# A four-block state-space and expert layer on one core: decay denominators from TensorE, dt spread by DMA, sums inside the last pairs, matrices on VectorE

## What is computed

```python
dt = clip(softplus(dt_raw + dt_bias), 1e-4, 0.1)             # per token and head
A = (pi * sigmoid(theta_raw)) ** 2 ; kdamp = 0.5 * sigmoid(k_raw)   # per head and state
denom = 1.0 + dt * kdamp + dt ** 2 * A
v = (v - dt * A * y + dt * u * Bv) / denom
y = y + dt * v + dt * u * By
o = sum_n(y * Cy) + sum_n(v * Cv)
```

## Time and profile before

| what | us |
|---|---|
| median of 3 runs (549.52 to 549.85) | 549.67 |
| the profiled execution | 547.52 |
| its span, first to last instruction | 545.8 |
| busy: TensorE, VectorE | 444.1, 469.8 |
| busy: ScalarE, GpSimd | 252.1, 306.3 |

### The profile page before, as it was taken

One profiled execution on the slowest core, in us unless ns is written; L12 is line 12 of the kernel. 1 busy time (PEld: TensorE's weight loads), 2 busy tenths in 40 slices (PEclk: granted clock), 3 DMA queues, 4 the chain that ended last, 5 costly groups with the idle time before them and its releaser, 6 DMA issues. The chain is left out here.

```text
span 545.8 us, 9581 instructions
## 1 busy us (share of the span) xinstructions
PE 444.1 (81%) x3238; PEld 358.6 (66%) x3238; DVE 469.8 (86%) x1275; ACT 252.1 (46%) x489; POOL 306.3 (56%) x373
## 2 busy tenths in 40 slices
PE   5850159996979988896889968898789987998997
PEld 4740147885747667784657757687565766786886
DVE  5699989989999998989989998989989997789542
ACT  1551126563375525453546524454537542444363
POOL 2027867768508757668526657676553676778100
PEclk9995559998999969999979988998988997999999
DMA  7500000000000010000000000000000000000000
GB/s 224 153 0 0 1 1 2 1 2 1 0 1 1 1 40 1 1 1 2 1 0 2 0 21 1 1 2 2 0 1 0 2 0 21 2 1 1 2 11 10
DMA packets 8434, 7.06 MB, mean 13 GB/s; under 512 B 1593, under 2 KB 7618, under 8 KB 8258
## 3 DMA queue, kind: packets, MB, share of 16 engines
q1 hardware_dynamic: 8386, 6.46, 3.9%
HBM read 5.41 MB, written 1.05 MB: 12 GB/s over the span
## 5 line engine op out<-in xcount | busy, mean ns | idle before, releaser
L590 PE MATMUL BC<-xnT,winT 128*128 128x128 f32 x512 | 79.8, 306 | 50.8 <-ACT pr L893 29.7
L590 PEld LDWEIGHTS BC<-xnT,winT 128*128 128x128 f32 x512 | 70.4, 214 | 58.2 <-issue 31.0
L1616 POOL TENSOR_TENSOR big<-mm 128x256 f32<-128x256 f32 x64 | 50.3, 786 | 71.4 <-DVE mm L1345 71.4
L1648 POOL TENSOR_SCALAR uT<-uT,skipT 128x512 f32<-128x512 f32 x8 | 17.0, 2138 | 73.9 <-DVE w L1430 42.1
L1619 POOL TENSOR_TENSOR vt<-mm 128x256 f32<-128x256 f32 x64 | 58.1, 907 | 0.0
L542 PE MATMUL HB<-xnT,w 128*128 128x512 f32 x108 | 55.7, 645 | 1.9 <-ACT gtm L978 0.9
L1637 POOL TENSOR_TENSOR mm<-ab,pr 128x256 f32<-128x256 f32 x48 | 41.3, 881 | 20.4 <-ACT pr L893 20.2
L915 ACT ACTIVATE big<-GV 128x256 f32<-128x256 f32 x60 | 23.1, 385 | 62.3 <-PE GV L615 60.9
L612 PE MATMUL GV<-big,vt 128*128 128x128 f32 x256 | 44.0, 297 | 8.3 <-POOL vt L1619 8.3
L1343 DVE TENSOR_TENSOR mm<-BC,pr 128x512 f32<-128x512 f32 x64 | 44.2, 691 | 5.7
L612 PEld LDWEIGHTS GV<-big,vt 128*128 128x128 f32 x256 | 35.8, 202 | 14.1 <-POOL vt L1619 11.6
(11 more groups left out here) (225 smaller groups left out, 1179.1 us busy)
## 6 DMA issues: line engine op xcount, KB each, us to landing
xr<-in_x SPq DMA_DIRECT2D x4, 256.0 KB, 4.5
winT<-in_w_inT SPq DMA_DIRECT2D x1, 1024.0 KB, 5.6
w<-in_rw SPq DMA_DIRECT2D x1, 1024.0 KB
out<-xr SPq DMA_DIRECT2D x3, 256.0 KB, 2.6
taps<-in_dw_wT SPq DMA_DIRECT2D x1, 512.0 KB, 3.6
w<-in_sw SPq DMA_DIRECT2D x2, 128.0 KB
out<-xr SPq DMA_DIRECT2D x2, 128.0 KB, 1.8
winT<-in_w_inT SPq DMA_DIRECT2D x1, 130.0 KB, 2.7
```

The costliest lines, as they stand in the source:

```text
L590: last = pe.matmul(b[:, j * TS:(j + 1) * TS], winT[:, col:col + NS], xt, start=True, stop=True)
L1616: pool.tensor_tensor(wt[q % 8][:], m[:, 0], m[:, 3], ALU.add)
```

## The change

1. The transpose at F_ROWS takes dt and its square together: `dtts` holds (tile, {dt, dt squared}, head), one more VectorE operation squares dt, four transposes put them into 8 rows of 512 tokens, and ScalarE copies these into `rows8`.
2. For each head (F_DENS = 9 to 12, block 0 too) one matmul of 8 rows and 512 columns against `coef8` gives `kdamp*dt + A*dt*dt` on all 128 partitions. ScalarE takes the logarithm right from PSUM into `lden`. The products L1151 and L1146, the copies L830, L832 and L820, and the logarithm L842 are gone.
3. `coef8` is made once at the start: a transpose of kdamp and A (`kavec`), a mask, and four VectorE operations.
4. dt itself, which beta and alpha of blocks 1 to 3 read from `ab`, comes by DMA: SyncE writes the four rows to a DRAM buffer and reads them back to all partitions, four transfers of 256 KB. Block 0 still takes it from matmuls of identity columns, four of 512 columns, now after the denominators' four.
5. The constants move: the running sums to k = 14 and 15, `inverse_den` from k = 18 to 16, `running_den` and beta from 19 to 17, alpha from 21 to 19.
6. GpSimd's `matrices` is gone; VectorE does all 20 operations in every block, where it did 16 in blocks 1 to 3.

```diff
-MAT_OPS = 14
+MAT_OPS = 20
-F_INV, F_BETA, F_DEN, F_ALPHA = KP + 2, KP + 3, KP + 3, KP + 5
-
-(F_STATS, F_XN, F_XNT, F_LOGITS, F_EXP, F_LOG1P, F_ROWS, F_BCAST, F_LOG, F_SCAN, F_CENTRE) = (
-    0, 2, 3, 5, 6, 7, 8, 9, 13, 15, 17)
+F_INV, F_BETA, F_DEN, F_ALPHA = KP, KP + 1, KP + 1, KP + 3
+
+(F_STATS, F_XN, F_XNT, F_LOGITS, F_EXP, F_LOG1P, F_ROWS, F_DENS, F_SCAN, F_CENTRE) = (
+    0, 2, 3, 5, 6, 7, 8, 9, 14, 16)
...
+            def spread_dt(g):
+                sp.wait_ge(h_free, h_read_of("rows", g))
+                if g > 1:
+                    sp.wait_ge(ld_dt, 16 * NH * (g - 1))
+                sp.dma_start(dt_rows, rows8[0:NH]).then_inc(st_dt, 16)
+                sp.wait_ge(st_dt, 16 * g)
+                sp.wait_ge(fill, FILL_OPS * g)
+                sp.wait_ge(fill_p, POOL_FILL_OPS * g)
+                sp.wait_ge(mat_d, MAT_OPS * g)
+                for h in range(NH):
+                    sp.dma_start(view(ab, DTN + h * SL, (NH * SL, GT), (1, TS)),
+                                 dt_rows[h:h + 1].rearrange("o (c t) -> o c t", c=GT).broadcast_to([128, GT, TS]))\
+                        .then_inc(ld_dt, 16)
...
-                    pe.transpose(hb[0:KP, 0:TS], dtts[g % 2][:], ident[:]).then_inc(h_ready, 1)
+                    for c in range(GT):
+                        last = pe.transpose(hb[0:2 * NH, c * TS:(c + 1) * TS],
+                                            dtts[g % 2][:, c].rearrange("p i h -> p (i h)"), ident[:])
+                    last.then_inc(h_ready, 1)
...
-                    for c in range(GT):
-                        row = NH * c + h
-                        last = pe.matmul(hb[:, c * TS:(c + 1) * TS], ident[0:KP, row:row + 1].broadcast_to([KP, 128]),
-                                         dtr, start=True, stop=True)
+                    hb = h_bank("den", g, h)
+                    pe.matmul(hb[:], coef8[:, h, :], rows8, start=True, stop=True).then_inc(h_ready, 1)
...
+            for h in range(NH):
+                pe.matmul(DT0[h][:], ident[0:2 * NH, h:h + 1].broadcast_to([2 * NH, 128]), rows8,
+                          start=True, stop=True).then_inc(first_dt, 1)
...
-                    act.activation(den_of(h), hb[:].rearrange("p (c f t) -> p c f t", c=GT, f=2), ACT.Identity,
-                                   bias=kvec[:, h:h + 1], scale=avec[:, h:h + 1])
-                    act.activation(view(ab, DTN + h * SL, (NH * SL, GT), (1, TS)), by_tile(hb[:]), ACT.Copy)\
+                if 0 <= k - F_DENS < NH:
+                    hb = h_read("den", g, h)
+                    act.activation(den_of(h), hb[:].rearrange("p (c f t) -> p c f t", c=GT, f=2), ACT.Ln, bias=1.0)\
                         .then_inc(h_free, 1)
...
-            def denominators(g, h):
-                dve.wait_ge(h_free, h_read_of("bcast", g, h))
-                dve.tensor_tensor(den_of(h), den_of(h), view(ab, DTN + h * SL, (NH * SL, GT), (MID, 2), (1, MID)),
-                                  ALU.mult).then_inc(den_done, 1)
...
             def beta(g):
                 dve.wait_ge(inv_den, NH + g)
+                dve.wait_ge(ld_dt, 16 * NH * g)
...
-            def matrices(g):
-                pool.wait_ge(ab_done, g + 1)
-                pool.wait_ge(h_ready, h_read_of("sums", GT * g - 1))
-                link(pool.tensor_tensor(scr_x(0), c1(0, 1), c2(0, 0), ALU.mult))
-                link(pool.tensor_scalar(entry(0, "x", "x"), scr_x(0), -1.0, 1.0, ALU.mult, ALU.add))
-                link(pool.tensor_tensor(scr_x(0), c2(0, 1), entry(0, "x", "x"), ALU.mult))
-                pool.tensor_tensor(entry(0, "v", "x"), c2(0, 0), scr_x(0), ALU.add).then_inc(mat_p, 1)
...
-                    matrices(g + 1)
                     rstd_of(ln_index(LN2, g))
```

More of the change, by code:

```diff
@@ L124, in build @@
         theta = sb("theta", NS, NH)
-        avec = sb("avec", NS, NH)
-        kvec = sb("kvec", NS, NH)
+        kavec = sb("kavec", NS, 2 * NH)
+        kvec, avec = kavec[:, 0:NH], kavec[:, NH:2 * NH]
+        head_mask = sb("head_mask", 2 * NH, NH)
+        coef8 = sb("coef8", 2 * NH, NH, NS)
         sgt = sb("sgt", NS, 4 * NH)
@@ L147, in build @@
         rstd = sb("rstd", 128, GT)
-        dtts = [sb(f"dtt{i}", 128, KP) for i in range(2)]
+        dtts = [sb(f"dtt{i}", 128, GT, 2, NH) for i in range(2)]
         lden = sb("lden", NS, 2 * KP * MID)
@@ L204, in build @@
         einv = sb("einv", 128, GT)
-        cmp, tie = (t[:].rearrange("p (c e j) -> p c e j", c=GT, e=NE) for t in tf)
+        cmp, tie = (t.rearrange("p (c e j) -> p c e j", c=GT, e=NE) for t in tf)
         rank = sb("rank", 128, GT, NE)
@@ L245, in build @@
         inv_den, beta_done = sem("inv_den"), sem("beta_done")
-        first_dt, first_id = sem("first_dt"), sem("first_id")
-        mat_f, mat_p, mat_d, mat_e, step, conv, fill, fill_p = (sem(s) for s in
-            ("mat_f", "mat_p", "mat_d", "mat_e", "step", "conv", "fill", "fill_p"))
+        first_dt = sem("first_dt")
+        mat_d, step, conv, fill, fill_p = (sem(s) for s in ("mat_d", "step", "conv", "fill", "fill_p"))
         bc_ready, sq_done, vc_done, mul_done, wv_done = (sem(s) for s in
@@ L1246, in matrices @@
             def matrices(g, part):
                 def after(n):
-                    dve.wait_ge(mat_d, MAT_OPS * (g - 1) + n)
+                    dve.wait_ge(mat_d, MAT_OPS * g + n)
                 if part == 0:
                     dve.wait_ge(ab_done, g + 1)
-                    dve.wait_ge(wv_done, KP * g)
-                    dve.wait_ge(h_ready, h_read_of("sums", GT * g - 1))
+                    if g:
+                        dve.wait_ge(wv_done, KP * g)
+                        dve.wait_ge(h_ready, h_read_of("sums", GT * g - 1))
@@ L1269, in matrices @@
+                    for f in range(2):
+                        after(5 + f)
                         dve.tensor_tensor(scr(f, 0), c1(f, 1), scr(f, 1), ALU.mult).then_inc(mat_d, 1)
-                    after(6)
-                    dve.tensor_tensor(scr_x(1), c2(1, 1), entry(1, "x", "x"), ALU.mult).then_inc(mat_d, 1)
+                    for f in range(2):
+                        after(7 + f)
+                        dve.tensor_tensor(scr_x(f), c2(f, 1), entry(f, "x", "x"), ALU.mult).then_inc(mat_d, 1)
@@ L1279, in matrices @@
                     for f in range(2):
-                        after(10 + f)
+                        after(11 + f)
+                        dve.tensor_tensor(entry(f, "v", "x"), c2(f, 0), scr_x(f), ALU.add).then_inc(mat_d, 1)
+                    for f in range(2):
+                        after(13 + f)
                         dve.tensor_tensor(scr(f, 0), c2(f, 1), entry(f, "x", "v"), ALU.mult).then_inc(mat_d, 1)
                     for f in range(2):
-                        after(13 + f)
@@ L1483, in _ @@
             last.then_inc(taps_done, 1)
-            for k in range(F_XNT, F_BCAST):
-                front_early(0, k)
-            first_denominators(0)
-            for h in range(1, NH):
-                first_denominators(h)
-                head_sums(h - 1)
-            head_sums(NH - 1)
+            dve.wait_ge(cst_g, 1)
+            link(dve.tensor_tensor(head_mask[:], ident[0:2 * NH, 0:NH], ident[0:2 * NH, NH:2 * NH], ALU.add))
+            dve.wait_ge(coef_t, 1)
+            for h in range(NH):
+                last = dve.tensor_scalar(coef8[:, h, :], RR[0:2 * NH, 0:NS], head_mask[:, h:h + 1], None, ALU.mult)
+            last.then_inc(coef_done, 1)
+            for k in range(F_XNT, F_DENS):
+                front_early(0, k)
+            for h in range(NH):
+                head_sums(h)
             head_coefficients()
-            first_matrices()
+            for part in range(3):
+                matrices(0, part)
             for g in range(NG):
```

130 lines of the change are left out of this document (42 added, 88 removed).

## The result

The changed kernel takes 562.67 us (median of 6 executions, 561.51 to 566.59), the kernel before 549.72 beside it: a ratio of 1.0247 (1.0213 to 1.028). On a second chip it was 565.99 against 549.2, 1.0315 (1.0289 to 1.0341). It is slower, as forecast, but by 13 to 17 us and not by 6.8. The profiled execution is the longest of the six, 566.59.

A forecast was written before the change was run, and what follows sets the result against it. VectorE was busiest (469.8 of 545.8 us), with TensorE the bound in pairs 8 to 13. Start -0.7 plus three blocks of +2.5 gave +6.8 on 549.67: 556.5 us, range 540 to 563.

The forecast's parts named there:

- the steps at 3.55 a block: Tail of a block: from -0.9 us at the end of state(2) to +2.65 at residual(3), through the moved steps.
- The start: Start of block 0: denominators by wide matmuls, -0.7 us; bounds +0.7 at the slow clock throughout, -1.4 without waiting for TensorE.
- the clock rise "near 27.5": Start of block 0: TensorE's clock rises near 27.5 us, so the last bank comes near 29.3 and VectorE ends near 31.0.
- Pairs 8 to 14: Each block's pairs 8 to 14: TensorE bounds, most of VectorE's removed 4.2 us becomes waiting; -0.9 at state(2)'s end.
- The faster rival: Pairs 8 to 13: TensorE isn't the bound, so 5.4 us a block more is gained; 540.3 us, chance 0.20.
- DMA: Moving the dt rows through DRAM costs nothing: the transfers end by 124 us and beta starts at 138.24.
- The order of the tail: Last pair and tail: first sum ahead of pair 15, exponentials ahead of the norms copy, beta ahead of state(3); +2.65 us at residual(3).
- From the norms copy to the residual: Block 0's tail: norms copy at 137.5, first tail part by 141.6, state(3) ends at 141.8, residual at 146.6, +2.65 us.
- The sum leaves it out: Slow TensorE clock after the longer gaps ahead of gv(15) and the tail: considered, but not counted in the forecast.
- the clock rival: The clock falls in tile 3's tail, one slow stretch a block: 3 x 1.5 us more, 561.0 us, chance 0.12.
- The two readings that it rests on: Tail matmuls in the trace before the change: 2.8 us in a slow stretch, where the next tile's take 1.5.
- The matrices: All twenty operations on VectorE: -0.1 us a block, as router_max waits for TensorE; next scan +2.55, from 160.05 to 162.6.

The follow-up runs named there:

- old steps: The changed kernel with sums, exponentials, beta and alpha back at the steps of the kernel before: 541.83 us, ratio 0.9881; measured again 542.65 us, ratio 0.9879.
- TensorE kept busy: The changed kernel with 18 and 28 added TensorE transposes that compute nothing, after pair 15's products and before tile 3's tail: 558.28 us, ratio 1.0161.
- busy start: The changed kernel with the steps of before, and 34 instead of 18 idle TensorE transposes at the program's start: 538.92 us, ratio 0.9825.
- both additions: The changed kernel with the steps of before, plus idle TensorE transposes at the start and while it waits at each block's first pairs: 542.71 us, ratio 0.9883.

## Why the prediction was right or wrong

**Direction, and its reason: right.** I put the loss into the order of the last steps, and the experiments show it there: 24.2 us for the steps, against 7.4 that everything else brings. The size is another matter. I had the steps at 3.55 a block (from -0.9 to +2.65); they cost 8.1.

**The start, forecast -0.7: wrong, +0.36.** The step that failed is the clock rise "near 27.5". After the change:

```profile
16.72 7.16 PE L501 MATMUL HB<-tfs,coef 8*128 8x512 f32 x8 [0.72 <-issue]
23.68 3.62 PE L724 MATMUL BC<-tfs,ident 8*128 8x512 f32 x4
27.09 3.62 PE L724 MATMUL GV<-tfs,ident 8*128 8x512 f32 x4
30.64 3.78 PE L512 MATMUL HB<-xnT,taps 128*128 128x256 f32 x8
```

The sixteen records of 512 columns take 0.9 us each, and the convolution behind them starts slow as well; my upper bound (+0.7, slow throughout) was the nearer. I had taken the rise as due at a time. In the changed kernel TensorE was busy without a gap from 16.72 to 30.64 and, by the length of its records, the clock did not rise; it rose within the convolution, as it had before, and the convolution now comes 8 us later.

**Pairs 8 to 14, -0.9 at the end of state(2): right, -1.0** (125.00 for 125.99). TensorE was the bound, and VectorE's lost products became waits. The faster rival, 5.4 a block more, fell: with the old steps pair 5 to pair 15 is shorter by 1.0 in block 0 and by 1.4 in block 1, and the denominators' part of the whole is 4 to 5 us.

**DMA, nothing: right.** No wait of beta is ended by a DMA; a load of 256 KB lands in 4.2 us.

**The order of the tail: right, instruction for instruction, until the norms copy.** Pair 15's products ended at 129.45 (forecast 129.7), vt at 132.93 (133.1), beta started at 135.60 (135.9), the norms copy at 137.11 (137.5), state(3) ended at 140.80 (141.8).

**From the norms copy to the residual, forecast 146.6: wrong, 149.09.** This is the term of the sum that was mis-sized, +2.65 for +5.1 in block 0 (4.7 in blocks 1 and 2, their pairs 0 to 5 left aside). Two steps in it failed. First, "the power, ubar and the first part of the tail follow by 141.6": they took until 143.30, 6.2 us from the norms copy on where I had 4.1, since the power, du and ubar ran beside beta, the state and alpha (1.95, 0.67 and 1.06 us; with the old steps 1.64, 0.20 and 0.61), and L667 took 1.97 for 1.08. So it was this chain that the rest of the tail hung on, and not the end of state(3), from which I had counted. Second, "The sum leaves it out", of the clock. TensorE had nothing for the 3.98 us ahead of L650, which my own timing implied, and went to 1.2 GHz for the tail. The windows show a granted clock of 0.69 and then 0.50 behind that gap. The Trainium skill ("TensorE: Matmul & The Clock Gate", Part 1) has idleness throttle the clock, and this trace agrees. What I held against it, a clock of 1.00 through gaps of 1.6 us, was no argument for a gap of 4. With TensorE kept busy the tail was 2.1 shorter in block 0 and 0.5 in the others, and the whole kernel 4.7 to 8.5 us; what is left then, +9.9, is nearer to the +6.8 that I summed without the clock.

**The size of the clock rival, 1.5 a block, was too small as well.** The two readings that it rests on, 2.8 and 1.5, make 1.3, and block 0's tail lost 2.1 to the clock. It also priced the tail alone. The changed kernel enters blocks 1 and 2 in a phase in which the half clock lasts almost to pair 5: 2.85 and 2.82 in the profiled execution, about half of that in the second chip's trace. The kernel with the old steps has that half too (15.52 and 15.77 from pair 0 to pair 5), so the moved steps don't make it. That this phase is chance and not a fixed price of the rest of the change is argued from the spread between executions, not shown.

**The matrices, -0.1: wrong, by 0.6 to 1.4 a block.** I let `router_max` wait for TensorE and so gave away the gain. In the changed kernel that was right at one point: router_max comes 10.63 after the residual (forecast 10.55):

```profile
159.72 0.19 DVE L1359 TENSOR_TENSOR lg<-lg,rb 128x32 f32<-128x32 f32 x1 [1.55 <-ACT lg L967]
165.22 0.29 DVE L1263 TENSOR_TENSOR tpA<-start,big 128x128 f32<-128x128 f32 x1
```

But the stretch to the scan was longer in blocks 1 and 2 of the kernel before (16.59 and 16.90) than in block 0 (16.09), from which I had taken it for all three.

**Range and rivals.** 562.67 lies inside 540 to 563, at its very edge; on the second chip it was outside. The clock rival, to which I gave 0.12 and 561.0, was the nearest.

## What to carry to other kernels

Moving a step forward in a hand-written order moves it past others on each engine that it touches: follow the small copy that it now stands in front of (here 0.26 us of ScalarE) to the end of its chain, and ask what covered that chain before. If the new order makes TensorE's gaps longer, price the matmuls behind them at 1.2 GHz in the sum itself (here 1.97 us for 1.08), not as a rival; that the clock stood through a gap once is no promise, as the tails with TensorE kept busy showed. And test such a bundle in parts: with its steps left alone, this change would have been a gain of 1.2%.

## What was unexpected of the hardware

- Filling one gap of TensorE doesn't keep the clock: with 40 added transposes the slow stretch moved from pairs 0 to 3 to pair 3 and what follows, and the kernel gained nothing (0.9904 for 0.9881 and 0.9879).
- A GpSimd product of 128 x 4 took 2.01 us beside a VectorE product of 128 x 2048, and 0.20 without it; the 2.29 us of the VectorE product didn't grow. Beside a GpSimd product of 128 x 256 (1.26 us for 0.73) the same VectorE operation takes 2.81.
- In the first 30 us of the changed kernel's trace the windows show a granted clock of 1.00 while the records run at half speed (8 records of 512 columns in 7.16 us, 0.90 each, where the same products of the later blocks take 0.56 on average). In the trace of the busy start the same eight records take the same 7.16 us, and the windows show 0.50. The rows' lengths are to be trusted there.
- Products of 8 rows kept TensorE busy without a gap from 16.72 to 30.64 and the clock stayed low; in the kernel with both additions it even fell among them. In both traces it was back within the convolution, whose matmuls have 128 rows. Why it rose there and not before is open.
